# The second batch's closing assigns tokens to rows in two passes of eight tiles, where there was one of eight and two of four

## What is computed

```python
x = x + _layernorm(attention(_layernorm(x)))
x = x + _layernorm(ffn(_layernorm(x)))

# ffn, with E = 8 experts and H = 256 features
scores = jnp.einsum('bsh,eh->bse', x, gate_w)
chosen = jnp.argmax(scores, axis=-1)
onehot = jax.nn.one_hot(chosen, 8)
expert_out = jnp.einsum('bsh,efh->bsef', x, expert_w)
return x + jnp.einsum('bsef,bse->bsf', expert_out, onehot)
```

## Time and profile before

| what | value |
|---|---|
| median of three runs | 711.79 us (711.3 to 713.42) |
| the profiled execution's own time | 712.63 us |
| its span | 710.9 us |
| busy share: PE, DVE, ACT, POOL | 87%, 82%, 75%, 37% |
| closing stage of the second batch, up to the last `rowat` | about 590 to 632.2 us |
| expert stage | 633.8 to the end |

### The profile page before, as it was taken

One profiled execution on the slowest core, in us unless ns is written; L12 is line 12 of the kernel. 1 busy time (PEld: TensorE's weight loads), 2 busy tenths in 40 slices (PEclk: granted clock), 3 DMA queues, 4 the chain that ended last, 5 costly groups with the idle time before them and its releaser, 6 DMA issues.

```text
span 710.9 us, 21562 instructions
## 1 busy us (share of the span) xinstructions
PE 615.4 (87%) x8705; PEld 432.0 (61%) x8717; DVE 584.9 (82%) x1153; ACT 533.6 (75%) x870; POOL 262.0 (37%) x425
## 2 busy tenths in 40 slices
PE   4799788999989999878799799999999998558773
PEld 2677545666656666755576366666666667436662
DVE  4899959988898899898999589888888898967653
ACT  3389788888887888775798788788878887445552
POOL 3134443343334333001577423233233320445554
PEclk9599999999999999999999899999999999979996
DMA  5931188798978988311032688889888873119111
GB/s 169 291 101 41 31 153 157 139 177 167 170 145 161 175 160 164 92 60 59 31 89 77 139 158 153 156 157 163 153 158 158 162 139 121 54 68 310 66 57 46
DMA packets 60665, 92.88 MB, mean 131 GB/s; under 512 B 7057, under 2 KB 29844, under 8 KB 60566
## 3 DMA queue, kind: packets, MB, share of 16 engines
q0 software_dynamic: 35088, 66.13, 48.7%
q1 hardware_dynamic: 24902, 25.37, 12.3%
q10 hardware_dynamic: 576, 0.00, 0.0%
HBM read 15.87 MB, written 14.66 MB: 43 GB/s over the span
## 4 chain that ended last, share of the span: by engine, by line
PE 47%; DVE 25%; DMA 9%; issue 7%; ACT 7%; another core or an unknown queue 2%; POOL 2%; SPq 0%; POOLq 0%; DVEq 0%; ACTq 0%
PE banks L1524 16%; PE banks L1567 7%; PE banks L1566 6%; PE banks L1568 6%; DMA e_h<-e_f 6%; DVE e_l L1102 5%; PE banks L1344 5%; PE banks L1396 3%; DMA e_x<-x_all 2%; DVE x_all L1175 2%; ACT e_f L665 1%; DVE st L1188 1%; DVE e_l L962 1%; DVE e_l L971 1%
## 5 line engine op out<-in xcount | busy, mean ns | idle before, releaser
L665 ACT ACTIVATE e_f<-banks,nbias,c_ 128x1024 f32<-128x1024 f32 x172 | 200.4, 1201 | 55.8 <-PE banks L1524 49.1
L1102 DVE TENSOR_TENSOR e_l<-e_f,e_h 128x1024 f16<-128x1024 f32 x172 | 206.9, 1226 | 37.4 <-DMA e_h<-e_f 29.0
L1524 PE MATMUL banks<-q_T,k_T 128*128 128x512 f16 (+1 forms) x1024 | 215.3, 384 | 7.1 <-DVE e_l L962 3.9
L1568 PE MATMUL banks<-v_mm,e_l 128*128 128x65 f16 x2048 | 205.4, 191 | 0.0
L1568 PEld LDWEIGHTS banks<-v_mm,e_l 128*128 128x128 f16 x2048 | 189.8, 99 | 0.0
L467 POOL DMA_DIRECT2D e_h<-e_f x148 | 78.9, 533 | 190.4 <-PE banks L1568 141.8
L1566 PE MATMUL banks<-v_mm,e_h 128*128 128x65 f16 x1376 | 139.9, 192 | 4.5 <-DVE e_l L1102 2.5
L1566 PEld LDWEIGHTS banks<-v_mm,e_h 128*128 128x128 f16 x1376 | 127.6, 96 | 25.4 <-DVE e_l L1102 9.9
L1567 PE MATMUL banks<-v_mm,e_h 128*128 128x64 f16 x1376 | 140.1, 195 | 0.0
L1567 PEld LDWEIGHTS banks<-v_mm,e_h 128*128 128x128 f16 x1376 | 127.4, 97 | 11.8
L1102 DVE TENSOR_TENSOR e_l<-x_all,e_x 128x1024 f16<-128x1024 f32 x84 | 102.5, 1233 | 13.6 <-DMA e_x<-x_all 10.2
(11 more groups left out here) (296 smaller groups left out, 1189.0 us busy)
## 6 DMA issues: line engine op xcount, KB each, us to landing
e_h<-e_f POOLq DMA_DIRECT2D x148, 256.0 KB, 3.8
e_x<-x_all POOLq DMA_DIRECT2D x72, 256.0 KB, 4.3
x_all<-x SPq DMA_DIRECT2D x12, 512.0 KB, 4.1
rows_d<-e_x SPq DMA_DIRECT2D x1, 5180.0 KB, 24.3
k_T<-k_T SPq DMA_DIRECT2D x16, 256.0 KB, 3.6
k_T<-rows_d SPq DMA_DIRECT2D x15, 259.0 KB, 5.3
q_T<-rows_d SPq DMA_DIRECT2D x5, 259.0 KB, 7.3
x_all<-weT SPq DMA_DIRECT2D x2, 512.0 KB, 10.6
```

What stands on the lines that cost most here:

```text
L665: act.activation(whole[s % ALL % NEF], ps_S[s % ALL % 3], ACT.Exp, bias=bias_of(h, k // NT), scale=CESC).then_inc(s_E, 1)
L1102: dve.tensor_tensor(low[s % ALL % NLO], whole[s % ALL % NEF], high[s % ALL % NHI], ALU.subtract).then_inc(s_El, 1)
L1524: return pe.matmul(ps_S[s % ALL % 3][:, c * BANK:(c + 1) * BANK], k_T[rows, 1 - c if cross else c, h * N + j * P:h * N + (j + 1) * P], q_T ...
L1568: ins = pe.matmul(o, low[s % ALL % NLO][:, at], v[:, 0:DH + 1], start=False, stop=j == NT - 1, skip_group_check=True)
```

## The change

The list of passes has one entry less. The pass over groups 2 and 3 (tiles 8 to 15) of the second batch is done at the end of pair 7, where there was one over group 2 at the end of pair 5 and one over group 3 at the end of pair 7.

```diff
-    PASSES = [(0, 0, 4), (1, 0, 2), (1, 2, 3), (1, 3, 4)]
+    PASSES = [(0, 0, 4), (1, 0, 2), (1, 2, 4)]
```

## The result

The changed kernel takes 720.36 us (median of four runs, 717.46 to 721.73) beside 712.34 us for the kernel before (median of four runs); the ratio is 1.011 with an interval of 1.008 to 1.014. The forecast was 0.9 us faster and its range ended at 715.5 us, so both were wrong. What happened has the mechanism of rival B, at more than twice its price. The profiled execution took 719.26 us with a span of 717.5 us, 6.6 us over the span before. At 604 us, ahead of the edit, its trace already stands 0.45 us behind the one before; that has to be taken off where times of the two traces are compared.

The account below looks back on a forecast made before the run. VectorE was taken to bound the second batch's closing, with a ScalarE pause of no known releaser, and TensorE the expert stage. -1.06 + 0.42 - 0.27 = -0.91 us from 711.79 gives 710.9 us; range 706.8 to 715.5 us.

Parts of the forecast that it names:

- rival B: Expert stage, double pages 0 to 3: ScalarE pauses once more under POOL's unbroken train, +3.6 us, 715.4 us; chance 0.20.
- `choose` of group 2: VectorE, 614.83 to 615.89 us: its removal starts the residual of pair 5 1.06 us earlier.
- If it belongs to that place in the program it moves with it: -1.06: ScalarE's 6.48 us pause ahead of the squares of pair 7 was taken to come 1.06 us earlier.
- the fetch: Instruction fetches in the DMA rows within the half microsecond where ScalarE's pause begins; the reason for taking -1.06 us.
- Rivals A: ScalarE's pause ahead of pair 7 ends where it did; +0.15 us is left, 711.9 us; chance 0.17.
- C: ScalarE's pause ahead of pair 7 shrinks; without it 704.6 us, with half of it 707.7 us; chance 0.16.
- C's half case: Half of ScalarE's pause ahead of pair 7 stays: 711.79 - 0.91 - 3.2 = 707.7 us, called the likelier.
- The wider instructions: Last pass on VectorE: thirteen instructions in `choose` and `page` get 64 numbers per partition for 32, +0.42 us.
- the table: VectorE's table has 32 marks for 40; of its two large instructions only the second counts, -0.27 us.
- So the longer train costs 0, and its slack falls from 6.0 us to 1.0 us.: Eight scatters in a row on POOL delay double page 4's load 4.03 us, still 1.0 us ahead of TensorE's need.
- Its "against": Reason given against a new ScalarE pause: from 638.76 us on, eight output scatters in one train brought none.

Follow-up runs that it names:

- landed_early: Kernel before, with GpSimd waiting for landings ahead of tiles 4, 8, 12 of the second batch, the first output scatter and double pages 2 and 4 only: 717.11 us, ratio 1.006.
- ring_parts: Computation left out: TensorE, ScalarE, VectorE pass a token in eight phases, varying TensorE's load and POOL's DMA train; the train of 8 has one wait of 4.11 us.

## Why the prediction was wrong

- `choose` of group 2: as said. The residual of pair 5 stands right behind the gate scores, with no `choose` between.
- "If it belongs to that place in the program it moves with it: -1.06" is wrong, and so is the fetch beside it as a reason. The pause didn't keep its length: it ended at 621.62 us for 625.56, 3.9 us earlier. It had ended 2.5 us after the start of the tenth scatter of a train (623.10 us); the edit left that train eight (the last at 621.02 us). The kernel parted at tile 8 shows the same without the edit. The Trainium skill, page "Runtime: NRT & Kernel Launch", section "Instruction fetch mechanics", had spoken against the fetch, and the runs agree: a train of DMAs moved the pause, 3.62 for 6.48 us with ScalarE's program as it was. Rivals A (end fixed) and C (pause shrinks) stood on the same wrong footing; C's half case describes this part: its sum puts the last `rowat` 3.8 us earlier (1.06 - 0.42 + 3.2), and it came 3.5 us earlier, 4.0 us from the same start. C's time is wrong all the same, as it had no price for the longer train.
- The wider instructions and the table: the table's took 1.20 us as forecast. The second still stands on the chain, now ahead of the `y_l` that TensorE waits for. The eight scatters came 1.28 us apart as said (one took 1.40 us), the last 2.4 us before the forecast 640.71.
- **The step that failed: "So the longer train costs 0, and its slack falls from 6.0 us to 1.0 us."** Its slack for the load did hold: double page 4's transposes follow the fillers at 652.38 us with no wait. But I priced the train only by what queues behind it. It costs while it runs: 2.47 + 5.18 us of pauses on ScalarE, then TensorE idle for 6.30 us and its next matmuls at the lower clock, together 4.6 us late at double page 4 although 3.5 us had been gained ahead of it. The unmerged kernel with only this train lost 7.7 us.
- Rival B had this mechanism, with 0.20 and 715.4 us. Its "against" was mistaken: "eight output scatters in one train" were two trains of four, with 1.49 us between them, after 1.10 us ahead of the first. And its price was one pause of the smaller size, where two came, with the clock's fall behind them. Both readings of the earlier trace rows shared the cause, and that should have raised the chance: two pauses, both under trains, and nothing else common. The row of POOL before the change that the "against" missed:
```profile
645.93 0.98 POOL L481 DMA_INDIRECT out<-e_l,k_T  x1 [1.49 <-DVE e_l L881]
```

## What to carry to other kernels

Where GpSimd issues indirect DMAs in rows, count how many go without a gap while another engine waits on TensorE: moving them together can cost several us although every transfer is hidden. When a pause has no releaser, or names TensorE, look at whether the matmuls that it waits for had long ended, and what another engine was doing from its start to its end. A wait that breaks a train is no sure cure, as it delays the issuer and so makes the next train longer (8.91 us here); breaks must lie where the issuer has slack up to the end, and be measured in more than one set of runs, since one set here showed no hold at all.

## What the runs showed of the hardware

- ScalarE went on up to 12.0 us after the end of the matmuls that it waited for (665.52 to 677.47 us in `landed_early`, 8.9 us of it a pause), in the ring up to 6.1 us (23.37 to 29.50 us in `ring_parts`, in a wait of 7.60 us). The Trainium skill, page "TensorE: Matmul & The Clock Gate", section "The cost: per-tile semaphore tail", gives a formula for the tail of matmuls packed in tiles; for one tile and one increment it comes to 56 ns, by an estimate from that formula. The traces agree outside the trains, where the squares follow the matmuls by 0.03 to 0.27 us, and not inside them.
- A hold ends either within a train (636.15 us in the changed kernel) or 0.5 to 3.5 us after the start of its last DMA (668.41 us in the kernel before, 111.15 us in `ring_parts`). What in the chip holds the increments stays open, and so do why ScalarE begins to wait only four to nine DMAs into a train and why two trains of eight gave none.
- One of the five sets had no hold, and there the kernel before took 698.11 us; in the others its medians are 709.98 to 713.21 us. The chips of the five sets are numbered 3, 13, 2, 0 and 13 on record: the set without holds and the last one, with holds, bear the same number. So it is not shown that the hold depends on the chip (the number alone doesn't say whether the two are one chip), and what sets that set apart stays open. The busy ring was not run in it.
